# Value and query projections moved into the heads, and half of the output projection moved ahead of the last context, in a four-sample attention and RWKV kernel

## The reference

```python
# block 0: 32 query heads of 16, 8 key/value groups, keys and values from ctx
q = x @ Wq + bq;  k = ctx @ Wk + bk;  v = ctx @ Wv + bv
attn = softmax(q k^T * scale + mask)              # 512 x 512 per head
x = layernorm(attn @ v @ Wo + bo + x) * gamma + beta
# block 1: 16 heads of 32
x = x + attention(ln1(x), ln1(x), mask 1) @ w_ao + b_ao      # self
x = x + attention(ln2(x), ctx, mask 2) @ w_co + b_co         # cross
x = x + gelu(ln3(x) @ w1 + b1) @ w2 + b2
# blocks 2 and 3: RWKV time mixing and channel mixing
```

## Time and profile before

| what | us |
| --- | --- |
| median of three runs | 4369.45 (4360.58 to 4370.68) |
| the profiled execution | 4371.74, of which the span in the trace is 4369.8 |
| PE busy | 3802.8 (87%) |
| DVE busy | 2631.0 (60%) |
| ACT busy | 2290.0 (52%) |
| POOL busy | 1688.0 (39%) |
| one sample, from the first scores of attention 0 to those of the next sample | 1134.09 to 2223.16 |
| its first scores of attention 1, of attention 2 | 1346.62, 1489.39 |

### The profile page before, as it was taken

One profiled execution on the slowest core, in us unless ns is written; L12 is line 12 of the kernel. 1 busy time (PEld: TensorE's weight loads), 2 busy tenths in 40 slices (PEclk: granted clock), 3 DMA queues, 4 the chain that ended last, 5 costly groups with the idle time before them and its releaser, 6 DMA issues. The chain is left out here.

```text
span 4369.8 us, 65250 instructions
## 1 busy us (share of the span) xinstructions
PE 3802.8 (87%) x23680; PEld 2348.6 (54%) x23680; DVE 2631.0 (60%) x5803; ACT 2290.0 (52%) x4528; POOL 1688.0 (39%) x1869
## 2 busy tenths in 40 slices
PE   7889899888888989988888998898888888889897
PEld 4444555555544455555654545555565444655555
DVE  5765646656576564565657656466566775546655
ACT  5665734434566563443466756344346575634444
POOL 4544542222454454222245445422224644542222
PEclk9999999998899999989989999998989999999898
DMA  4032210102203221010220322101022132210102
GB/s 132 15 118 63 73 67 30 58 20 97 72 16 117 63 73 67 30 58 20 97 73 25 107 63 82 58 30 58 20 97 76 40 90 69 76 58 30 58 30 97
DMA packets 94554, 276.01 MB, mean 63 GB/s; under 512 B 25472, under 2 KB 25984, under 8 KB 73088
## 3 DMA queue, kind: packets, MB, share of 16 engines
q1 hardware_dynamic: 94208, 271.58, 19.3%
HBM read 201.24 MB, written 4.19 MB: 47 GB/s over the span
## 5 line engine op out<-in xcount | busy, mean ns | idle before, releaser
L806 POOL TENSOR_SCALAR probs<-probs,row_inv 128x512 f32<-128x512 f32 x1024 | 693.1, 693 | 641.0 <-DVE row_inv L721 641.0
L665 ACT ACTIVATE probs<-probs,row_max 128x512 f32<-128x512 f32 x1024 | 733.4, 725 | 131.8 <-DVE row_max L737 130.4
L560 PE MATMUL ps<-ident,probs 128*128 128x128 f32 x4096 | 610.3, 290 | 176.8 <-ACT pT L659 150.9
L560 PEld LDWEIGHTS ps<-ident,probs 128*128 128x128 f32 x4096 | 480.6, 147 | 386.3 <-ACT pT L659 215.6
L370 PE MATMUL ps<-mix,wring 128*128 128x512 f32 x1024 | 485.3, 612 | 36.4 <-DMA wring<-in_blocks_dram 36.4
L659 ACT ACTIVATE pT<-ps 128x512 f32<-128x512 f32 x768 | 431.0, 602 | 113.7 <-PE ps L560 113.3
L535 PE MATMUL ps<-kstack,qstack 96*128 96x512 f32 (+1 forms) x1024 | 378.3, 464 | 16.4 <-DMA qstack<-hi 7.3
L737 DVE CUSTOM_DVE_ANT_0 probs<-ps,maskA 128x512 f32<-128x512 f32 x512 | 329.4, 681 | 43.3 <-PE ps L535 43.3
L737 DVE CUSTOM_DVE_ANT_0 probs<-ps,neg 128x512 f32<-128x512 f32 x512 | 340.6, 685 | 8.8
L370 PEld LDWEIGHTS ps<-mix,wring 128*128 128x128 f32 x1024 | 196.4, 195 | 235.7 <-issue 188.5
L1550 POOL TENSOR_TENSOR hinv<-hvar,minus_half 128x32 f32<-128x32 f32 x24 | 146.2, 6093 | 289.4 <-DVE hvar L1260 289.4
(11 more groups left out here) (179 smaller groups left out, 7339.8 us busy)
## 6 DMA issues: line engine op xcount, KB each, us to landing
wring<-in_blocks_dram SPq DMA_DIRECT2D x151, 1024.0 KB, 5.2
qstack<-hi SPq DMA_DIRECT2D x256, 64.0 KB, 2.0
kstack<-hi SPq DMA_DIRECT2D x256, 64.0 KB, 2.0
maskA<-in_mask_dram SPq DMA_DIRECT2D x9, 1024.0 KB, 7.6
rows<-in_rows_dram SPq DMA_DIRECT2D x8, 1024.0 KB, 4.6
qstack<-hi SPq DMA_DIRECT2D x256, 32.0 KB, 2.0
qstack<-lo SPq DMA_DIRECT2D x128, 64.0 KB, 2.0
kstack<-lo SPq DMA_DIRECT2D x128, 64.0 KB, 2.0
```

The lines of the kernel that those rows point to most:

```text
L560: ins = nc.tensor.transpose(tile[:, qc * P:(qc + 1) * P], probs[:, m % PSLOTS, qc, kc * P:(kc + 1) * P], ident[:, :])
L665: nc.scalar.activation(p, p, ACT.Exp, bias=row_max[:, n % PSLOTS, qc:qc + 1], scale=-1.0, accum_out=row_sum[:, n % PSLOTS, qc:qc + 1]).the ...
L806: nc.gpsimd.tensor_scalar(p, p, row_inv[:, (n - 1) % PSLOTS, qc:qc + 1], 1.0, ALU.mult, ALU.mult)\
```

## The change

1. `pe_values` becomes `pe_v`, one value tile, in halves if wanted. `Attention.projects` is a table from a round to the tile that is projected in it: in attentions 1 and 2 value tiles 0 to 3 in rounds 0 to 3, query and key of group 2 in rounds 4 and 5, of group 3 in rounds 8 and 9; in attention 0 query tiles 2 and 3 in rounds 2 and 5. The half tiles stand behind the transposes of each half round. ACT's and POOL's splits follow the table. DVE empties a value tile at the end of its round.
2. The value projections ahead of the heads of attentions 1 and 2 go, with DVE's part of them.
3. The output projection is summed in banks 0 to 3. Context chunk 0 is multiplied in at the end of round `heads`, chunk 1 at the end of round `heads + 1`, each for all four token tiles; chunks 2 and 3 follow the last context.

```diff
-        def to_N(pe, tile, w, src, tc, n=H, base_=0, fin=None, ready=None):
+        def to_N(pe, tile, w, src, tc, n=H, base_=0, fin=None, ready=None, fcs=range(C)):
...
-            for fc in range(C):
+            for fc in fcs:
...
+                self.projects = {n: ('v', n) for n in range(C)} | {4: ('q', 2), 5: ('k', 2), 8: ('q', 3), 9: ('k', 3)}
+                if self.shared:
+                    self.projects = {2: ('q', 2), 5: ('q', 3)}
...
-        def pe_values(pe, A, tiles=range(C)):
-            w_wait(pe, A.vblk)
-            for tc in tiles:
-                to_N(pe, take(pe, 'v', A.tag, tc), weights(A.vblk), A.src, tc, n=A.vcols, base_=A.voff,
-                     fin=tile_ready.reach('v', A.tag, tc))
+        def pe_v(pe, A, tc, fcs=range(C), tile=None):
+            if tc == 0 and 0 in fcs:
+                w_wait(pe, A.vblk)
+            tile = take(pe, 'v', A.tag, tc) if tile is None else tile
+            to_N(pe, tile, weights(A.vblk), A.src, tc, n=A.vcols, base_=A.voff, fcs=fcs,
+                 fin=tile_ready.reach('v', A.tag, tc) if C - 1 in fcs else None)
+            return tile
...
-                pe_values(pe, A)
-                pe_queries(pe, A, (1, 2, 3))
+                for tc in range(C):
+                    pe_v(pe, A, tc)
+                pe_queries(pe, A, (1,))
...
-                pe_values(pe, A)
             if t == 2:
                 pe_queries(pe, A)
-                pe_values(pe, A, (2, 3))
...
-                    if not A.shared and g + 2 < A.groups and i < 2:
-                        part = (pe_q, pe_k)[i](pe, A, g + 2, fcs=(2 * half, 2 * half + 1), tile=None if half == 0 else part)
-
-            w_wait(pe, A.oblk)
+                    if A.heads <= n < A.heads + LAG and half == 1:
+                        fc = n - A.heads
+                        if fc == 0:
+                            w_wait(pe, A.oblk)
+                        pe.wait_ge(*act_done.when('context', t, fc))
+                        for tc in range(C):
+                            if fc == 0:
+                                pe.wait_ge(*(S['scores_taken'] if A.shared else dve_done).when(*(() if A.shared else ('sm',)), t, A.heads - 1, tc))
+                            to_N(pe, ps[:, tc, :], weights(A.oblk), oT, tc, fcs=(fc,))
+                    if n in A.projects:
+                        kind, c = A.projects[n]
+                        part = {'q': pe_q, 'k': pe_k, 'v': pe_v}[kind](pe, A, c, fcs=(2 * half, 2 * half + 1),
+                                                                       tile=None if half == 0 else part)
+
             for tc in range(C):
-                to_N(pe, take(pe, 'out', t, tc), weights(A.oblk), oT, tc, fin=tile_ready.reach('out', t, tc),
+                to_N(pe, ps[:, tc, :], weights(A.oblk), oT, tc, fcs=(2, 3), fin=tile_ready.reach('out', t, tc),
...
-            for g in range(4 if A.shared else 2):
+            for g in range(2):
                 act_split(act, A, 'q', g)
...
-                    if step == 's' and not A.shared and g + 2 < A.groups and i < 2:
-                        act_split(act, A, 'qk'[i], g + 2)
+                    if step == 's' and A.projects.get(n, 'v')[0] != 'v':
+                        act_split(act, A, *A.projects[n])
...
-            if t < 2:
+            if t == 0:
                 dve_values(dve, A, range(C))
...
+                if A.projects.get(n, 'q')[0] == 'v':
+                    dve_values(dve, A, (A.projects[n][1],))
...
-                if not A.shared and g + 2 < A.groups:
-                    if i == 1:
-                        pool_split(pool, A, 'q', g + 2)
-                    if i == 2:
-                        pool_split(pool, A, 'k', g + 2)
+                if A.projects.get(n - 2, 'v')[0] != 'v':
+                    pool_split(pool, A, *A.projects[n - 2])
...
                     pe_k(pe, A2, 1)
-                    pe_values(pe, A2, (0, 1))
                     pe_norm_turn(pe, 'ln2', xn)
```

More of the change, by code:

```diff
@@ L380, in to_N @@
                 m = nc.tensor.matmul(tile[:, 0:n], src[:, fc, tc * P:(tc + 1) * P],
-                                     w[:, fc * H + base_:fc * H + base_ + n], start=(fc == 0), stop=(fc == C - 1))
-            m.then_inc(*fin)
+                                     w[:, fc * H + base_:fc * H + base_ + n], start=(fc == 0), stop=(fc == C - 1),
+                                     skip_group_check=(len(fcs) < C))
+            if C - 1 in fcs:
+                m.then_inc(*fin)
         def dve_stats(dve, tag, tc):
@@ L675, in act_attention @@
                     nc.scalar.activation(oT[:, c, :], ps[:, OBANK, :], ACT.Copy).then_inc(*act_done.reach('context', t, c))
-                for step in (('x0', 'e0', 'x1', 'e2', 'x2', 'x3') if A.shared else ('e0', 'e1', 'x0', 'x1', 'e2', 'e3', 'x2', 'x3', 's')):
-                    if step == 's' and not A.shared and g + 2 < A.groups and i < 2:
-                        act_split(act, A, 'qk'[i], g + 2)
+                for step in (('x0', 'e0', 'x1', 'e2', 'x2', 'x3', 's') if A.shared else ('e0', 'e1', 'x0', 'x1', 'e2', 'e3', 'x2', 'x3', 's')):
+                    if step == 's' and A.projects.get(n, 'v')[0] != 'v':
+                        act_split(act, A, *A.projects[n])
                     if step[0] == 'e' and 0 <= m < A.heads:
@@ L689, in dve_values @@
             t = A.tag
-            if t < 2:
+            if t < 2 and 0 in tiles:
                 dve.wait_ge(sems['rows_in'], 16 * (t + 1))
@@ L776, in residual @@
             dve.wait_ge(*tile_ready.when('out', t, tc))
-            nc.vector.tensor_tensor(x[:, tc, :], ps[:, ring.bank('out', t, tc), :], x[:, tc, :], ALU.add)\
+            nc.vector.tensor_tensor(x[:, tc, :], ps[:, tc, :], x[:, tc, :], ALU.add)\
                 .then_inc(*dve_emptied.reach('out', t, tc))
@@ L1693, in _ @@
                     dve_norm(dve, 'ln2', xn, lambda tc: residual(dve, 1, tc))
-                    dve_values(dve, A2, range(C))
                     dve_attention(dve, A2)
```

## The result

The changed kernel takes **4552.6 us** (median of four runs, 4546.9 to 4555.9), the kernel before, on the same chip, 4366.3; the ratio is **1.042, interval 1.0411 to 1.0437**. The forecast was 4533, its own range 4500 to 4570: the direction and the mechanism held, and the sum was 20 us short. The profiled execution, 4546.9 us, is the lowest of the four.

The account below looks back on a forecast made before the run. VectorE was taken to bound quiet rounds and PE those with a projection. Attentions 0, 1 and 2 add 6.9, 15.4 and 18.7 us, 41.0 per sample, 164 for four: 4369.45 becomes 4533 us, range 4500 to 4570 (8 in 10: 4460 to 4600).

Parts of the forecast that it names:

- VectorE bounds quiet rounds, PE those with a projection: Attention 1's rounds: DVE busy 5.03 us of about 5.10 in quiet rounds; PE has 6.1 us of work with a projection.
- Start of attention 1: Without value tiles ahead of the heads, first scores wait only for group 0's last copy: -3.3 us per sample.
- Rounds 0 to 3: Value tiles in attentions 1 and 2: 2.6 half clock, 0.7 VectorE in round 1, 2.4 in rounds 2 and 3; +5.7 us.
- Round 4: Attentions 1 and 2: starts without PE's lead from quiet rounds, 6.2 instead of 5.61 us; +0.6 (0 to 1).
- The copies' distance: Groups 2 and 3 copied later, so rounds 8 and 12 each stop 2.7 us; +5.4 us for both (0 to 10).
- Rounds 8 to 10 with their half clock: Attentions 1 and 2: rounds 8 to 10 like 4 to 6, +5.0 us; half clock behind both stops, +2.0.
- Attention 2, "the same as attention 1": Attention 2 priced with attention 1's terms, without the gain at its start: 18.7 us per sample.
- Attention 0: Start -2.1, query 2 in round 2 +4.6, query 3 in round 5 +3.0, k1's load +1.4: 6.9 us per sample.
- Tails, 0 each: Output projection steps moved ahead: last normalised tile at 1461.9 against 1461.54, so 0 per tail (-2.3 to +3.4).
- the copies are in time: Rival: POOL's low part or SP ends 3 us sooner, stops and their half clock go; 4474 us, chance 0.13.
- everything fits: Rival: projections fit PE's idle time, copies in time; 4329 us with tails gaining (0.05), 4370 without (0.05).
- Half clock throughout: Rival: PE falls to half clock at every wait and returns slowly; 56 us per sample, 4593 us, chance 0.12.

Follow-up runs that it names:

- experiment 4: Changed kernel plus matmuls nobody reads while PE waits for copies: 4589.4 us; with fewer ahead of the first scores of attentions 1 and 2, 4536.1 us.
- experiment 1: Changed kernel with SP's load of weight block o2 moved behind attention 2's copies of group 3: 4538.7 us.
- experiment 6: Kernel before with only the output projection's part of the change, 4372.7 us; then also POOL's low part of up_0 moved behind ln3's rstd, 4383.9 us.
- the last run of experiment 6: Kernel before with the output projection's part of the change, and POOL's low part of weight block up_0 moved behind ln3's rstd: 4383.9 us.
- tails alone: Kernel before with only the output projection's part of the change, in all three attentions: 4372.7 us, ratio 1.0003 to 1.0029.

## Why the forecast was right, and what was mis-sized

- **VectorE bounds quiet rounds, PE those with a projection**: right. Value rounds 5.7 to 6.65, rounds 9 and 10 7.46 and 6.70 (7.55 and 6.70 in the earlier trace rows).
- **Start of attention 1**, -3.3: measured -4.5. The step itself was right: the first scores stood 4.8 to 5.5 us behind the start of the last of the 24 issues and stand 2.05 behind it now, with the landing at 2.0 in both. What lies outside that term moved too. PE projects queries and keys in 13.9 to 14.0 us and not in 15.2 to 15.35, at full clock from the start (1.00 for the first 3 us; 0.51 before); the 24 copies take 15.1 us and not 15.6 to 16.4; attention 0's tail takes 0.85 back.
- **Rounds 0 to 3, +5.7**: 25.0 against 20.5 us and 0.2 ahead of the first maximum, 4.6. Half clock was about 1.2 of it (experiment 4; 1.7 in attention 2), not 2.6. **Round 4, +0.6**: +0.85.
- **The copies' distance**: the chain was worked out at 22.25 us from the key's scores to round 8's; it is 22.41 (1417.39 to 1439.80). The two stops are 3.3 and 3.4 us, not 2.7: the first maximum too comes later behind the wait, at half clock. **Rounds 8 to 10 with their half clock, 5.0 + 2.0**: 6.8, and nothing behind round 12 (5.11). In all, attention 1's heads +18.9 where the terms gave 18.7.
- **Attention 2, "the same as attention 1"**: this is the step that failed, 24.1 instead of 18.7, about 21 us of the kernel. The two starts that came 1.2 and 2.4 us earlier than forecast hide part of it, so that the traces differ by 174.5 us where 164 was forecast; the other 9 us of the miss are spread of the runs about their medians. That the sum came so near is in part luck. About 3.7 us of the 5.4 are o2's load (experiment 1). It stands ahead of late copies as k1's load does in attention 0, which I priced; here I took attention 1's price, where the load at that place, o1's, waits only for the query. The other 1.6 lie before round 8: four copies of the query's low part take SP 3.81 us there and not 2.49, as one of them is issued beside a transfer of instructions (last section).
- **Attention 0**: start -2.1, measured -2.1 (from the start of the last issue to the scores, 4.2 us before and 2.0 after). Rounds +9.0, measured +8.8, but by luck, as two errors cancel. The query tiles cost 5.5 and not 7.6: for query 2, priced at 4.6, round 2 grows by 3.1 and round 3 shrinks by 1.0 in the mean, which leaves 2.1. The load costs 3.5 and not 1.4, since its delay lengthens two rounds, 7 and 8, and not one, and in one sample of the four 9 and 10 too.
- **Tails, 0 each**: right in attention 1 at equal clock. Attention 0 pays 0.85; attention 2 1.1 to 3.5, 2.1 in the mean, because I followed PE and VectorE to the last normalised tile and not POOL, whose 4.6 us weight part now stands across the first `rstd`. That attention 2's first scores come 2.4 us earlier was priced at 0; it hangs on where half clock and the transfers of instructions fall (experiment 6).
- The rivals: "the copies are in time" and "everything fits" are out by the sixteen stops. "Half clock throughout" asked for 6 us more per attention; the restarts cost less than the forecast's 2.6 + 2.0 (3.6 and 3.1, at least).

## What to carry to other kernels

Moving a projection later moves its copies (here the stops of 3.3 and 3.4 us before rounds 8 and 12 of attention 1), and every load that waits for its last use, in the DMA queue's order (k1's load 3.5 us per sample, o2's 3.7); work out for each group the distance from the part to its first reader, and for each queue what stands between. An engine's idle share in a quiet stretch is not room: a value tile there cost its evacuation on the bounding engine, 0.69 us of VectorE, and more: the four cost 6.3 and 7.8 us in attentions 1 and 2, and the early start that they bought was worth less, 4.5 and 2.0 us. Where two stages look alike, compare the lists of their queues before one's price is taken for the other.

## What the hardware did that was not expected

- A VectorE normalisation that reads and writes SBUF (128x512 f32) took 4.87, 4.87, 4.71 and 4.71 us in the four samples of the last run of experiment 6, where it begins just behind the start of POOL's weight part (4.49 to 4.66 us); alone it takes 0.51 to 0.55. VectorE's residual additions, which read PSUM, kept their 0.69 us beside the same POOL instruction (tails alone). Why the normalisation takes so long there, no run shows.
- SP issues copies at 0.62 us each, but some single ones take 1.1 to 1.9 us, so that a group of four takes up to 3.81 us and not 2.49. They go with transfers of the queue q8, which the page lists as "instruction". In the changed kernel 29 of the 1248 copies take over 1 us to issue, and 28 of these overlap such a transfer by more than 50 ns; of the other 1219, 12 do. Before it is 34 of 35 and 13 of 1213. In attention 2 one of these transfers starts at the copies for group 2 in all four samples (1586.39 in the second, beside the 3.81 us), and the 24 copies take 16.3 to 16.6 us; in attention 1 none falls on an issue, and they take 15.1. Where they fall differs from kernel to kernel: the 24 copies ahead of attention 1's first scores take 15.1 us in the changed kernel, 15.6 to 16.4 before, and 16.1 to 16.5 with the added matmuls of experiment 4. No run sets these transfers on purpose, so this is shown as a coincidence in every trace and not as a cause.
- The same tail, instruction for instruction, lasted 25.9 or 27.6 to 28.3 us, by whether half clock fell into its transposes: over the 7 us behind the last maximum the mean clock was 1.00 in the first and 0.76 in the second (experiment 6). Ahead of it PE was busy for 10.1 of 12 us in both.
